# Shifting x in its DMA, loading feed-forward weights during attention, and a layer loop that begins in the feed-forward

## The chip, the cores and the metric

One of the eight cores of a Trainium2 chip runs the kernel. The metric is the device time of one execution in microseconds (us). The kernel before took 2393.64 us (median of three runs, 2389.98 to 2394.75).

## The reference, cut to what matters

x has 16 batches of 128 tokens with 128 features. A cross-attention, a mixture of experts and a second cross-attention come first. The last stage runs six transformer layers; it takes 1840 of the 2383 us, and all that the change touches is there:

```python
def shift_tokens(t):                       # second half of the features comes from the token before
    a, s = jnp.split(t, 2, -1)
    s = jnp.pad(s, ((0, 0), (1, 0), (0, 0)))[:, :-1]
    return jnp.concatenate([a, s], -1)
def attn_layer(x, Wqkv, qs, ksc, Wo):      # 16 heads of 64
    q, k, v = jnp.split(x @ Wqkv, 3, -1)
    q, k = l2norm(q) * qs, l2norm(k) * ksc
    q, k = rotary(q), rotary(k)            # with a scale by position
    return local_attention(q, k, v) @ Wo   # windows of 32, each looks at itself and the window before
def ffn_layer(x, g, bln, W1, b1, W2, b2):
    a, gate = jnp.split((layernorm(x) * g + bln) @ W1 + b1, 2, -1)
    return a * gelu(gate) @ W2 + b2
for i in range(6):
    x = attn_layer(shift_tokens(x), Wqkv[i], q_scale[i], k_scale[i], Wo[i]) + x
    x = ffn_layer(shift_tokens(x), ln_g[i], ln_b[i], W1[i], b1[i], W2[i], b2[i]) + x
```

## The kernel before

The tokens of one batch lie on the 128 partitions; Y holds all 16 batches. The program of each engine is written out by hand, and the engines meet at semaphores only.

**Attention.** A unit is one batch and four heads, 64 units to a layer. A Pipeline (L48) runs the stages of an engine by slots: in slot c, a stage with skew s works on unit c - s, in the order of the list of stages (for TensorE L903: scores, turn_qk, pv, project_qk, project_v, output, turn_o, turn, turn_x). start(...) writes out slots 0 to 7 of a layer, steady() is a hardware loop of seven rounds of eight slots (L73), and finish(...) writes out the last slots. So a layer has 56 slots in the loop and the rest written out.

**x.** For each batch the SyncE queue copies one batch of Y into xin[:, k], k = 0 or 1 (take_x, L363). In slot 4b TensorE turns it (l_turn_x, L796) with two matmuls, each against 64 columns of the array: L802 the first half of the features against the identity, L803 the second half against shift_t, which moves each token one on. It first waits for the copy of v (L1179, ScalarE), which reads the same PSUM bank. ScalarE (L1155) and VectorE (L1571) split the result in two, and the projections (L814, L823) of the next slot read that.

**Values.** ScalarE writes the v of a unit to l_v (L1179). move_values (L349) copies pieces of it to other partitions with four DMAs for two units (L360); pv (L878) of the first of these two units waits for them, some four slots later.

**SyncE's order in a layer** (serve_layer, L372): for each batch move_values for two units, next_x, move_values for the other two. During batches 0 to 2 it loads the six pieces of the next layer's Wqkv. After batch 15 it loads Wo, waits for the first feed-forward group, takes x of batches 0 and 1 for the next layer, waits until the whole feed-forward is done (L400), loads the feed-forward weights of the next layer with twelve DMAs (L335 to L347) and goes back to move_values of batch 0. All of these stand in one queue.

**Feed-forward.** Four groups g of four batches: shift (L919, L920), statistics, normalise (L1653), turn_n (L928), three pairs of hidden matmuls (L944, L945), gelu (L1227), the gated product (L1663), output (L955), residual (L1670). Group 0 begins between the slots of finish(...), and slots 0 to 7 of the next layer's attention (nxt.start) are placed between and after groups 2 and 3. The copy of layer n + 1's first x therefore happens inside the feed-forward of layer n.

**The loop over layers.** On each engine a hardware loop runs layers 0 to 4 (L585 POOL, L1020 TensorE, L1282 ScalarE, L1746 VectorE, L411 SyncE), and its body is rest_of_layer: steady, finish, the feed-forward, nxt.start. It goes back after slot 7 of the next layer, so that the jump lands on that layer's steady(). Layer 5 is written out after the loop: between it and layer 4 no jump is taken. The loop jumps back four times.

Of the kernel before, what the change touches and what calls it, by code (L numbers as in the profile page):

```python
# [90 lines left out]
def build(nc, t, out):  # L91
    with ExitStack() as ctx:
# [193 lines left out]
        def _(sp):  # L286
# [76 lines left out]
            def take_x(ly, b, k):  # L363

                sp.dma_start(xin[:, k], one(Y, b)).then_inc(ld_xin[k], 16)
# [6 lines left out]
            def serve_layer(ly, last):  # L372

                for b in range(4):
                    for q in range(2):
                        move_values(ly, b, b % 2, q)
                        if q == 0:
                            next_x(ly, b, b % 2)
                        if not last and 2 * b + q < W_CHUNKS:
                            if b + q == 0:  # L380
                                sp.wait_ge(l["w_split"], upto(0, (ly + 1) * W_CHUNKS))
                                apart(sp)
                            load_projections(ly + 1, 2 * b + q)
                with sp.Fori(2, B // 2 - 1) as i:
                    for k in range(2):
                        move_values(ly, 2 * i + k, k, 0)
                        next_x(ly, 2 * i + k, k)
                        move_values(ly, 2 * i + k, k, 1)
                for b in range(B - 2, B):
                    for q in range(2):  # L390
                        move_values(ly, b, b % 2, q)
                if not last:
                    sp.wait_ge(l["out_done"], upto(0, (ly + 1) * B))
                    apart(sp)
                    load_output(ly + 1)
                    sp.wait_ge(f["y_done"], upto(0, ly * 4 + 1))
                    apart(sp)
                    for b in range(2):
                        take_x(ly + 1, b, b)
                    sp.wait_ge(f["y_done"], upto(0, (ly + 1) * 4))  # L400
                    apart(sp)
                    load_feed_forward(ly + 1)
# [3 lines left out]
            load_feed_forward(0)  # L406
# [16 lines left out]
        def _(pool):  # L423
# [5 lines left out]
            pool.memset(l_ss[:, :, :, 1:], 1e-24).then_inc(preset, 1)  # L429
# [126 lines left out]
            def feed_forward(ly):  # L556
                fb = ly * 4
                pool.wait_ge(ld_fw, (ly + 1) * (16 * FW_DMAS))
                for g in range(4):
# [11 lines left out]
            def rest_of_layer(ly, att, nxt):  # L571

                att.steady()
                att.finish(0, 1, 2, 3)
                feed_forward(ly)
                if nxt is not None:
                    nxt.start(*range(UNROLL))
# [6 lines left out]
            first.start(*range(2, UNROLL))  # L584
            with pool.Fori(0, LAYERS - 1) as ly:  # L585
                rest_of_layer(ly, attention(ly), attention(ly + 1))
            rest_of_layer(LAYERS - 1, attention(LAYERS - 1), None)


        @block.tensor  # L590
        def _(pe):
# [180 lines left out]
            def attention(ly):  # L772
# [23 lines left out]
                def l_turn_x(u, b, j):  # L796

                    if j % 4 == 0:
                        x = xin[:, j // 4]
                        pe.wait_ge(ld_xin[j // 4], (ly * B + b - j // 4) * 8 + 16)  # L800
                        values_read(l_turn_x, b, 0)
                        pe.matmul(bank[0:HALF, 1, 256:384], x[:, 0:HALF], ident, start=True, stop=True)  # L802
                        pe.matmul(bank[HALF:, 1, 256:384], x[:, HALF:], shift_t, start=True, stop=True)\  # L803
                          .then_inc(l["x_turned"], 1)
# [101 lines left out]
            def feed_forward(ly, last):  # L906
# [54 lines left out]
            def rest_of_layer(ly, att, nxt):  # L961


                shift, turn_n, hidden, output = feed_forward(ly, nxt is None)
# [10 lines left out]
                att.finish(6)  # L975
                for g in range(4):
# [8 lines left out]
                    hidden(g, 1)  # L985
# [33 lines left out]
            first.start(*range(3, UNROLL))  # L1019
            with pe.Fori(0, LAYERS - 1) as ly:  # L1020
                rest_of_layer(ly, attention(ly), attention(ly + 1))
            rest_of_layer(LAYERS - 1, attention(LAYERS - 1), None)


        @block.scalar
        def _(act):
# [205 lines left out]
            def rest_of_layer(ly, att, nxt):  # L1232

# [7 lines left out]
                att.finish(6)  # L1241
                for g in range(4):
# [4 lines left out]
                    gelu(g, 1)  # L1247
# [33 lines left out]
            first.start(*range(3, UNROLL))  # L1281
            with act.Fori(0, LAYERS - 1) as ly:  # L1282
                rest_of_layer(ly, attention(ly), attention(ly + 1))
            rest_of_layer(LAYERS - 1, attention(LAYERS - 1), None)


        @block.vector
        def _(dve):
# [385 lines left out]
            def rest_of_layer(ly, att, nxt):  # L1674

                stats, norm, gated, residual = feed_forward(ly)
# [9 lines left out]
                att.finish(6)  # L1686
                for g in range(4):
# [6 lines left out]
                    if g < 3:  # L1694
# [50 lines left out]
            first.start(*range(3, UNROLL))  # L1745
            with dve.Fori(0, LAYERS - 1) as ly:  # L1746
                rest_of_layer(ly, attention(ly), attention(ly + 1))
            rest_of_layer(LAYERS - 1, attention(LAYERS - 1), None)


# [58 lines left out]
```

## Time and profile before

| | |
|---|---|
| median of three runs | 2393.64 us |
| profiled execution, its own time | 2385.23 us |
| its span, first to last instruction | 2383.4 us |
| mean granted TensorE clock | 0.968 |
| six layers | 545.8 to 2383.4 us |

A layer takes some 307 us from its first projection to the next layer's; 56 slots in the loop take some 211 of them. TensorE is busy for 93% of the span. In the chain of work that ended last, 74% is TensorE's and 4% is time in which an engine waited for nothing that the profile shows ("issue"). In the rows below, "2.44 <-DVE f_n" in brackets is idle time of the engine before the instruction, and what ended it. PE is TensorE's matmul, PEld its weight load, and SPq the queue of SyncE. A matmul in float32 shows as two instructions (x2); a transpose shows as one.

### The profile page before, as it was taken

To read this page: it belongs to the slowest core of one execution; us is meant where nothing else is said; L and a number is where in the kernel's file an instruction comes from. 1 tells how busy PE (TensorE), PEld (TensorE's weight loads), DVE (VectorE), ACT (ScalarE), POOL (GpSimd) and SP (SyncE) were. 2 spreads that over 40 slices of the span, in tenths; PEclk is the share of its full clock that TensorE was granted. 3 is DMA by queue.
4 is the path that set the end of the run, shared out by engine and by line. 5 is a ranking of instruction groups with operands and counts; after the bars stand their busy time and mean duration, and the time that the engine had idled before them with its cause. 6 is when DMAs were issued, how large, how long until landed. Compare 5 with 4: busy or idle time off the path is not lost.

```text
span 2383.4 us, 105405 instructions
## 1 busy us (share of the span) xinstructions
PE 2211.0 (93%) x36645; PEld 1694.9 (71%) x36645; DVE 1725.2 (72%) x4617; ACT 1563.0 (66%) x5192; POOL 1412.3 (59%) x2638
## 2 busy tenths in 40 slices
PE   6998699998999979999799998999988999889998
PEld 4775277776888658886578875788756888578885
DVE  4777788886777657786577865677756788568884
ACT  3554455565888548886478873788746888468883
POOL 3443611115888538885378863688726888278882
PEclk9998899998999989999999999999998999999999
DMA  3000000011111112111111111211102111021110
GB/s 98 0 0 1 0 1 0 0 48 43 49 39 40 31 42 54 40 40 33 43 50 40 40 29 34 63 40 39 34 21 71 40 39 38 14 50 40 40 38 22
DMA packets 107749, 82.51 MB, mean 35 GB/s; under 512 B 26422, under 2 KB 100292, under 8 KB 107588
## 3 DMA queue, kind: packets, MB, share of 16 engines
q1 hardware_dynamic: 107588, 80.46, 12.9%
q8 instruction: 89, 1.46, 0.3%
q14 instruction: 72, 0.59, 0.1%
HBM read 21.94 MB, written 1.05 MB: 10 GB/s over the span
## 4 chain that ended last, share of the span: by engine, by line
PE 74%; DVE 4%; issue 4%; SPq 2%; ACT 1%; POOL 1%; DMA 0%; DVEq 0%; ACTq 0%; POOLq 0%
PE bank L814 14%; PE bank L831 9%; PE bank L898 7%; PE bank L878 6%; PE bank L858 6%; PE bank L823 6%; PE bank L888 4%; PE bank L841 3%; PE bank L850 2%; PE bank L749 2%; PE bank L955 2%; PE bank L944 2%; PE bank L945 2%; PE bank L738 2%; PE bank L597 1%
## 5 line engine op out<-in xcount | busy, mean ns | idle before, releaser
L530 POOL TENSOR_TENSOR l_qk<-l_rot 128x512 f32<-128x512 f32 x384 | 494.4, 1287 | 134.0 <-PE bank L831 60.6
L1202 ACT ACTIVATE l_qkT<-bank 128x512 f32<-128x512 f32 x384 | 229.8, 599 | 278.2 <-PE bank L831 278.2
L1580 DVE TENSOR_TENSOR l_rot<-bank,l_tab 128x512 f32<-128x512 f32 x384 | 265.0, 690 | 197.8 <-ACT l_sq L1186 197.8
L551 POOL TENSOR_TENSOR l_qk<-l_qk,l_rn 128x512 f32<-128x512 f32 x384 | 400.9, 1044 | 0.9
L1166 ACT ACTIVATE prob<-bank,peak 128x64 f32<-128x64 f32 x1536 | 355.0, 322 | 1.3 <-DVE peak L1602 1.3
L814 PE MATMUL bank<-w_high,xs_part 128*128 128x512 f32 x768 | 351.8, 458 | 3.2 <-DVE xs_part L1571 2.8
L1186 ACT ACTIVATE l_sq<-bank 128x512 f32<-128x512 f32 x384 | 237.1, 617 | 55.9 <-PE bank L814 44.8
L1584 DVE TENSOR_TENSOR l_rot<-bank,l_tab 128x512 f32<-128x512 f32 x384 | 261.5, 681 | 0.0
L831 PE MATMUL bank<-const,l_qk 128*128 128x128 f32 x1536 | 255.2, 289 | 5.3 <-POOL l_qk L551 5.2
L1594 DVE TENSOR_REDUCE l_ss<-l_sq 128x8 f32<-128x512 f32 x384 | 259.8, 677 | 0.2
L898 PE MATMUL bank<-l_wo,l_oT 128*128 128x128 f32 x1536 | 239.0, 279 | 0.0
L823 PE MATMUL bank<-w_high,xs_part 128*128 128x256 f32 x768 | 202.9, 286 | 11.6 <-issue 11.6
L878 PE MATMUL bank<-l_v,probT 64*32 64x65 f32 x4608 | 179.5, 225 | 35.2 <-DMA stash<-l_v 22.8
L898 PEld LDWEIGHTS bank<-l_wo,l_oT 128*128 128x128 f32 x1536 | 206.3, 193 | 3.3 <-issue 0.3
L1602 DVE TENSOR_REDUCE peak<-bank 128x4 f32<-128x256 f32 x384 | 160.8, 419 | 50.7 <-PE bank L858 43.4
L831 PEld LDWEIGHTS bank<-const,l_qk 128*128 128x128 f32 x1536 | 163.5, 142 | 41.4 <-POOL l_qk L551 6.8
L878 PEld LDWEIGHTS bank<-l_v,probT 64*32 64x32 f32 x4608 | 117.2, 108 | 105.3 <-issue 105.3
L814 PEld LDWEIGHTS bank<-w_high,xs_part 128*128 128x128 f32 x768 | 146.8, 191 | 62.2 <-issue 5.8
L435 POOL TENSOR_SCALAR ln_rs<-ln_mv 128x1 f32<-128x1 f32 (+1 forms) x64 | 14.5, 227 | 273.5 <-DVE ln_mv L1548 128.3
L858 PE MATMUL bank<-l_qkT 64*32 64x64 f32 x12288 | 175.8, 223 | 0.0
L878 PE MATMUL bank<-stash,probT 64*32 64x65 f32 x7680 | 174.5, 226 | 0.0
L1619 DVE TENSOR_TENSOR o<-bank,rsum 128x256 f32<-128x256 f32 x384 | 163.1, 425 | 13.3
(202 smaller groups left out, 5374.8 us busy)
## 6 DMA issues: line engine op xcount, KB each, us to landing
stash<-l_v SPq DMA_DIRECT2D x768, 65.0 KB, 2.0
early<-in_L_ffn_Wqkv_dram SPq DMA_DIRECT2D x36, 256.0 KB, 3.2
xin<-Y SPq DMA_DIRECT2D x96, 64.0 KB, 1.8
l_wo<-in_L_ffn_Wo_dram SPq DMA_DIRECT2D x6, 512.0 KB, 3.8
f_w<-in_L_ffn_W_dram SPq DMA_DIRECT2D x6, 341.0 KB
out_dram<-X SPq DMA_DIRECT2D x4, 256.0 KB, 2.3
f_w<-in_L_ffn_W_dram SPq DMA_DIRECT2D x6, 128.0 KB
l_oT<-in_L_xattn_Wkv_dram SPq DMA_DIRECT2D x1, 512.0 KB, 6.1
```

The source lines that it names most:

```text
L530: pool.tensor_tensor(l_qk[:, k], l_rot[:, k, 0], l_rot[:, k, 1], ALU.add).then_inc(l["add_done"], 1)
L551: pool.tensor_tensor(v, v, l_rn[:, k, :, None].broadcast_to([128, 8, L_DIM]), ALU.mult).then_inc(l["qk_done"], 1)
L814: ins = pe.matmul(bank[:, 0, :].rearrange("p (q n) -> p q n", q=2), xs_part[:, part, j // 4], w[:, 0:2, 256 * g:256 * g + 256], start=n == ...
L823: ins = pe.matmul(bank[:, 1, 0:256], xs_part[:, part, j // 4], w[:, 2, 256 * g:256 * g + 256], start=n == 0, stop=n == 2)
L831: ins = pe.transpose(bank[:, 2, n * 128:(n + 1) * 128], l_qk[:, j % 2, n * 128:(n + 1) * 128], ident)
L858: ins = pe.matmul(bank[w * WINDOW:(w + 1) * WINDOW, 3 + r, BAND * p:BAND * (p + 1)], l_qkT[rows, j % 2, queries:queries + WINDOW], l_qkT[r ...
L878: ins = pe.matmul(bank[w * WINDOW:(w + 1) * WINDOW, 6 - p, at:at + L_DIM + 1], probT[rows, j % 2, 128 * r + w * WINDOW:128 * r + (w + 1) * ...
L898: ins = pe.matmul(bank[:, 7, 256:384], l_oT[:, j // 4, p], l_wo[:, p], start=p == 0, stop=p == 7, skip_group_check=True)
L1166: ins = act.activation(prob[:, k, n * BAND:(n + 1) * BAND], bank[:, 3 + r, p * BAND:(p + 1) * BAND], ACT.Exp, bias=peak[:, k, n:n + 1])
L1580: dve.tensor_tensor(l_rot[:, k, 0].rearrange("p (q h n) -> p q h n", q=2, h=4), bank[:, 0, :].rearrange("p (q h n) -> p q h n", q=2, h=4), ...
L1584: dve.tensor_tensor(l_rot[:, k, 1].rearrange("p (q h s n) -> p q h s n", q=2, h=4, s=2), bank[:, 0, :].rearrange("p (q h s n) -> p q h s n ...
L1594: dve.tensor_reduce(l_ss[:, k, :, 0], l_sq[:].rearrange("p (h n) -> p h n", n=L_DIM), AX.X, ALU.add)\
```

## The change

It has three parts.

- take_x copies the two halves of the features with a DMA each, and the second half goes to the partition after its own: the shift is done by the DMA. Partition 0 of that half is set to zero once (POOL). l_turn_x becomes one transpose of 128 x 128.
- load_feed_forward(ly) is taken from the end of the layer before (and from the prologue) and stands behind batch 3 of the same layer. The wait for the end of the feed-forward stands before batch 2.
- rest_of_layer is cut in two on TensorE, ScalarE, VectorE and POOL: into_feed_forward (steady, finish and the first part of group 0) and out_of_feed_forward (the rest, and nxt.start). Layer 0's into_feed_forward is written out ahead of the loop; the loop's body is out_of_feed_forward(ly) and into_feed_forward(ly + 1), five rounds; layer 5's out_of_feed_forward follows. The order of the work on each engine stays; the jump back now comes after hidden(0, 1), gelu(0, 1), norm(1) and POOL's part of group 0. SyncE's loop over layers stays where it is.

ScalarE's part of the diff has the same form as TensorE's and is left out.

```diff
@@ -362,7 +362,10 @@
-                sp.dma_start(xin[:, k], one(Y, b)).then_inc(ld_xin[k], 16)
+                x = one(Y, b)
+                sp.dma_start(xin[:, k, 0:HALF], x[:, 0:HALF]).then_inc(ld_xin[k], 16)
+                sp.dma_start(xin[1:, k, HALF:], x[0:S - 1, HALF:]).then_inc(ld_xin[k], 16)
@@ -372,6 +375,9 @@
                 for b in range(4):
+                    if b == 2:
+                        sp.wait_ge(f["y_done"], upto(0, ly * 4))
+                        apart(sp)
                     for q in range(2):
@@ -381,6 +387,7 @@
                             load_projections(ly + 1, 2 * b + q)
+                load_feed_forward(ly)
                 with sp.Fori(2, B // 2 - 1) as i:
@@ -397,13 +404,9 @@
                         take_x(ly + 1, b, b)
-                    sp.wait_ge(f["y_done"], upto(0, (ly + 1) * 4))
-                    apart(sp)
-                    load_feed_forward(ly + 1)
             load_output(0)
-            load_feed_forward(0)
             sp.wait_ge(c["y_done"], upto(0, 2))
@@ -426,7 +429,8 @@
             pool.memset(m_p[:, :, EXPERTS:], -1.0)
-            pool.memset(l_ss[:, :, :, 1:], 1e-24).then_inc(preset, 1)
+            pool.memset(l_ss[:, :, :, 1:], 1e-24)
+            pool.memset(xin[0:1, :, HALF:], 0.0).then_inc(preset, 1)
             pool.wait_ge(preset, 1)
@@ -553,10 +557,9 @@
-            def feed_forward(ly):
+            def feed_forward(ly, *groups):
                 fb = ly * 4
-                pool.wait_ge(ld_fw, (ly + 1) * (16 * FW_DMAS))
-                for g in range(4):
+                for g in groups:
                     yg = Y[:, 4 * g:4 * g + 4, :]
@@ -568,11 +571,14 @@
-            def rest_of_layer(ly, att, nxt):
+            def into_feed_forward(ly, att):
                 att.steady()
                 att.finish(0, 1, 2, 3)
-                feed_forward(ly)
+                pool.wait_ge(ld_fw, (ly + 1) * (16 * FW_DMAS))
+                feed_forward(ly, 0)
+            def out_of_feed_forward(ly, nxt):
+                feed_forward(ly, 1, 2, 3)
                 if nxt is not None:
@@ -582,9 +588,11 @@
             first.start(*range(2, UNROLL))
+            into_feed_forward(0, first)
             with pool.Fori(0, LAYERS - 1) as ly:
-                rest_of_layer(ly, attention(ly), attention(ly + 1))
-            rest_of_layer(LAYERS - 1, attention(LAYERS - 1), None)
+                out_of_feed_forward(ly, attention(ly + 1))
+                into_feed_forward(ly + 1, attention(ly + 1))
+            out_of_feed_forward(LAYERS - 1, None)
@@ -794,14 +802,10 @@
                     if j % 4 == 0:
-                        x = xin[:, j // 4]
-                        pe.wait_ge(ld_xin[j // 4], (ly * B + b - j // 4) * 8 + 16)
+                        pe.wait_ge(ld_xin[j // 4], (ly * B + b - j // 4) * 16 + 32)
                         values_read(l_turn_x, b, 0)
-                        pe.matmul(bank[0:HALF, 1, 256:384], x[:, 0:HALF], ident, start=True, stop=True)
-                        pe.matmul(bank[HALF:, 1, 256:384], x[:, HALF:], shift_t, start=True, stop=True)\
-                          .then_inc(l["x_turned"], 1)
+                        pe.transpose(bank[:, 1, 256:384], xin[:, j // 4], ident).then_inc(l["x_turned"], 1)
@@ -903,7 +907,7 @@
-            def feed_forward(ly, last):
+            def feed_forward(ly):
@@ -958,10 +962,8 @@
-            def rest_of_layer(ly, att, nxt):
-                shift, turn_n, hidden, output = feed_forward(ly, nxt is None)
+            def into_feed_forward(ly, att):
+                shift, turn_n, hidden, _ = feed_forward(ly)
                 att.steady()
@@ -973,6 +975,10 @@
                 att.finish(6)
+                hidden(0, 1)
+            def out_of_feed_forward(ly, nxt):
+                shift, turn_n, hidden, output = feed_forward(ly)
                 for g in range(4):
@@ -982,7 +988,7 @@
                         output(g - 1)
-                    hidden(g, 1)
+                        hidden(g, 1)
                     if g == 3 and nxt is not None:
@@ -1017,9 +1023,11 @@
             first.start(*range(3, UNROLL))
+            into_feed_forward(0, first)
             with pe.Fori(0, LAYERS - 1) as ly:
-                rest_of_layer(ly, attention(ly), attention(ly + 1))
-            rest_of_layer(LAYERS - 1, attention(LAYERS - 1), None)
+                out_of_feed_forward(ly, attention(ly + 1))
+                into_feed_forward(ly + 1, attention(ly + 1))
+            out_of_feed_forward(LAYERS - 1, None)
...
@@ -1671,9 +1684,8 @@
-            def rest_of_layer(ly, att, nxt):
-                stats, norm, gated, residual = feed_forward(ly)
+            def into_feed_forward(ly, att):
+                stats, norm, gated, _ = feed_forward(ly)
                 att.steady()
@@ -1684,6 +1696,10 @@
                 att.finish(6)
+                norm(1)
+            def out_of_feed_forward(ly, nxt):
+                stats, norm, gated, residual = feed_forward(ly)
                 for g in range(4):
@@ -1691,7 +1707,7 @@
                         gated(g, 0)
-                    if g < 3:
+                    if 0 < g < 3:
                         norm(g + 1)
@@ -1743,9 +1759,11 @@
             first.start(*range(3, UNROLL))
+            into_feed_forward(0, first)
             with dve.Fori(0, LAYERS - 1) as ly:
-                rest_of_layer(ly, attention(ly), attention(ly + 1))
-            rest_of_layer(LAYERS - 1, attention(LAYERS - 1), None)
+                out_of_feed_forward(ly, attention(ly + 1))
+                into_feed_forward(ly + 1, attention(ly + 1))
+            out_of_feed_forward(LAYERS - 1, None)

```

## Rows read from the trace of the kernel before

**Rows 1.** The page, part 1: busy time, share, instructions of each engine.

```profile
PE 2211.0 (93%) x36645; PEld 1694.9 (71%) x36645; DVE 1725.2 (72%) x4617; ACT 1563.0 (66%) x5192; POOL 1412.3 (59%) x2638
```

**Rows 2.** Two stretches: engines' busy time, TensorE's clock, DMA share, GB/s.

```profile
930.00:960.00 30.00, 29.83 (x680) 24.11 (x679) 23.96 (x60) 24.37 (x90) 24.51 (x49) 1.00 0.15 40
...
874.00:878.00 4.00, 3.68 (x44) 3.19 (x44) 1.43 (x5) 1.36 (x5) 0.18 (x1) 0.50 0.45 124
```

**Rows 3.** Chain that ended last, in layer 1: start, duration, what.

```profile
904.60 0.39 PE bank L878 x32
...
907.11 0.25 PE bank L802
...
908.67 0.39 PE bank L878 x32
...
912.27 0.39 PE bank L878 x32
```

**Rows 4.** Same stretch in order of time: ScalarE, TensorE's weight loads.

```profile
906.51 0.40 ACT L1179 ACTIVATE l_v<-bank 128x256 f32<-128x256 f32 x1
...
907.04 0.13 PEld L802 LDWEIGHTS bank<-const,xin 128*64 128x64 f32 x1 [0.17 <-ACT l_v L1179]
...
907.41 0.11 PEld L850 LDWEIGHTS bank<-l_mask,cbf 128*128 128x128 bf16 x2 [0.17 <-issue]
...
910.92 0.21 PEld L850 LDWEIGHTS bank<-l_mask,cbf 128*128 128x128 bf16 x2
```

**Rows 5.** The page's groups (busy, mean ns, idle), then the tile xin's landing.

```profile
L831 PE MATMUL bank<-const,l_qk 128*128 128x128 f32 x1536 | 255.2, 289 | 5.3 <-POOL l_qk L551 5.2
...
DMA to landing us min/median/max: 1.8/1.8/4.6
```

**Rows 6.** Waits of TensorE: total us, times, longest.

```profile
PE bank L878 <- DMA stash<-l_v: 22.8, 5, 4.9
...
PE bank L850 <- issue: 15.8, 4, 4.8
```

**Rows 7.** SyncE's queue in order of time, first boundary of layers.

```profile
862.77 0.35 SPq L336 DMA_DIRECT2D f_w<-in_L_ffn_W_dram  x1
...
870.28 1.15 SPq L360 DMA_DIRECT2D stash<-l_v  x2
```

**Rows 8.** TensorE in order of time at layer boundaries, and POOL's L551 there.

```profile
865.85 0.48 PE L814 MATMUL bank<-w_high,xs_part 128*128 128x512 f32 x1
...
874.32 0.28 PE L878 MATMUL bank<-l_v,probT 64*32 64x65 f32 x1 [4.90 <-DMA stash<-l_v]
...
894.10 0.50 PE L814 MATMUL bank<-w_high,xs_part 128*128 128x512 f32 x1
...
1786.99 0.48 PE L814 MATMUL bank<-w_high,xs_part 128*128 128x512 f32 x1
...
1814.61 0.50 PE L814 MATMUL bank<-w_high,xs_part 128*128 128x512 f32 x1
...
2094.27 0.48 PE L814 MATMUL bank<-w_high,xs_part 128*128 128x512 f32 x1
...
2107.45 0.50 PE L814 MATMUL bank<-w_high,xs_part 128*128 128x512 f32 x1
...
2115.16 0.50 PE L814 MATMUL bank<-w_high,xs_part 128*128 128x512 f32 x1
...
L551 POOL TENSOR_TENSOR l_qk<-l_qk,l_rn x4: 1039/1044/1051, 861.0 to 871.0; 128x512 f32<-128x512 f32 x4
```

**Rows 9.** In order of time: layer 0's feed-forward, ScalarE after its jump back.

```profile
821.17 0.66 PE L928 MATMUL bank<-const,f_n 128*128 128x128 f32 x4 [2.44 <-DVE f_n L1653]
...
825.90 1.06 PE L944 MATMUL bank<-f_nT,f_w 128*128 128x512 f32 x2
...
884.97 0.21 ACT L1192 ACTIVATE l_y<-l_s 128x8 f32<-128x8 f32 x1 [2.85 <-issue]
...
887.11 0.39 ACT L1179 ACTIVATE l_v<-bank 128x256 f32<-128x256 f32 x1 [1.94 <-issue]
```

More of the change, by code:

```diff
@@ L1241, in rest_of_layer @@
                 att.finish(6)
+                gelu(0, 1)
+            def out_of_feed_forward(ly, nxt):
+                copy_n, gelu = feed_forward(ly)
                 for g in range(4):
@@ L1246, in rest_of_layer @@
                         gelu(g, 0)
-                    gelu(g, 1)
+                        gelu(g, 1)
                     if g == 3 and nxt is not None:
@@ L1672, in feed_forward, with into_feed_forward @@
                 return f_stats, f_norm, f_gated, f_residual
-            def rest_of_layer(ly, att, nxt):
-                stats, norm, gated, residual = feed_forward(ly)
+            def into_feed_forward(ly, att):
+                stats, norm, gated, _ = feed_forward(ly)
                 att.steady()
@@ L1686, in rest_of_layer, with out_of_feed_forward @@
                 att.finish(6)
+                norm(1)
+            def out_of_feed_forward(ly, nxt):
+                stats, norm, gated, residual = feed_forward(ly)
                 for g in range(4):
@@ L1745, in _ @@
             first.start(*range(3, UNROLL))
+            into_feed_forward(0, first)
             with dve.Fori(0, LAYERS - 1) as ly:
-                rest_of_layer(ly, attention(ly), attention(ly + 1))
-            rest_of_layer(LAYERS - 1, attention(LAYERS - 1), None)
+                out_of_feed_forward(ly, attention(ly + 1))
+                into_feed_forward(ly + 1, attention(ly + 1))
+            out_of_feed_forward(LAYERS - 1, None)
 _INS = ["x", "ctx_1024", "L0_xattn_w_q", "L0_xattn_b_q", "L0_xattn_w_k", "L0_xattn_b_k", "L0_xattn_w_v",
```

## The prediction, made before the changed kernel was run

> **What bounds the kernel now.** I read the page first. TensorE is busy 2211.0 of 2383.4 us [rows 1], and in the middle of a layer it leaves no gap: 29.83 of 30 us, with the other engines at 24 to 24.5 [rows 2]. So there, and only there, each piece of TensorE's time that goes is time of the kernel. The chain that ended last gives the price of a slot. From one start of pv (L878) to the next it is 912.27 - 908.67 = 3.60 us; where the slot turns an x it is 908.67 - 904.60 = 4.07 us [rows 3]. Everything else is found where a layer meets the next. The list of TensorE's waits has two large entries there: L878 waits 22.8 us in 5 places for the DMAs that move v, and L850 waits 15.8 us in 4 places with nothing shown that it waits for [rows 6]. There are five boundaries of layers and four jumps back of the outer loop, and the second wait is the first matmul behind the jump. At the fifth boundary, where no jump is taken, it is absent.
>
> To price a boundary with all its after-effects I take TensorE's order of time from the projection of slot 5 to that of steady slot 1, four slots: 28.25 us at the first boundary (865.85 to 894.10), 27.62 at the fourth (1786.99 to 1814.61), the other two alike (28.29 and 28.14), and 20.89 at the fifth (2094.27 to 2115.16) [rows 8]. The two stalls are less than the excess, since TensorE comes out of them at its lower clock: 0.50 between 874 and 878 us, the 1.2 GHz level, after 4.9 us without a matmul [rows 2, 6].
>
> **Part 1, x is shifted by its DMA: the turn.** The 96 turns (16 batches, six layers) each cost 4.07 - 3.60 = 0.47 us [rows 3]. Where it goes, by the weight loads [rows 4]: an ordinary slot loads L850's weights at 910.92, right behind the last turn of prob. With an x, the load for L802 begins 0.20 us behind that turn's last matmul (906.84, the second of two 0.11 us apart; the same 0.20 in nearly every slot of the loop), the four matmuls take two passes of 0.11 us, as the halves run side by side, and L850's load begins 0.20 us behind the last of them. The view names ScalarE's copy of v as what ended the first gap, but that copy ends at 906.51 + 0.40 = 906.91, and the load comes 0.13 later; so I read both 0.20 as the price of changing from 128 x 128 to 128 x 64 and back. The Trainium skill ("TensorEngine Tiling (Array Packing)", Key Properties) says that a change of tiling mode drains TensorE. The trace agrees, with 0.20 us each way.
>
> A transpose is one instruction and one pass (1536 for 384 units of four [rows 5]) and needs no other shape. Bounds of the saving: 0.11 if both gaps stay and only a pass goes; 0.36 if the new turn costs just its pass. Between them stands the copy of v: it ends at 906.91, and the shortest distance from its end to the load in any turn is 0.05, so the load can begin at 906.96, 0.12 behind an unbroken stream. New price 0.11 + 0.12 = 0.23 us, saving 0.47 - 0.23 = 0.24 us. I take this, since both of its terms are read from the same slot. 96 x 0.24 = **23 us**, bounds 10 and 35.
>
> **Part 1, the DMAs.** Each x now needs two issues on SyncE, one more by about 0.5 us (L360 takes 1.15 for two [rows 7]), with lines of 256 bytes instead of 512. An x is issued some five slots ahead of its turn, 18 us, and lands in 1.8, at worst 4.6 us [rows 5]; even a landing three times as long is covered. The moves of v behind it in the queue are 0.5 us later and needed four slots (14 us) later; in steady slots SyncE has two slots, 7.2 us, for four moves (2.4 us) and two halves of x. Cost 0 for both. POOL's memset is in the prologue, where POOL waits: 0.
>
> **Part 2, feed-forward weights behind batch 3.** At a boundary SyncE waits for the last residual, then issues twelve DMAs from 862.77 on and only at 870.28 the first move of v [rows 7]; TensorE waits 4.90 us, until 874.32 [rows 8]. Afterwards nothing of the kind stands ahead: SyncE goes back as soon as it has issued x of batches 0 and 1, and finds v of units 0 and 1 copied at about 858.5. Four moves to 861 and 2.1 us to land make 863; TensorE wants them at 874.32 - 4.90 = 869.4. The stall goes at five boundaries. What is late next is POOL: it forms L551 for units 0 to 3 every (871.0 - 861.0) / 3 = 3.35 us [rows 8], back to back, and TensorE's slots 5 and 6 can't be shorter. So these two slots take 6.7 (POOL) to 7.2 us (twice 3.60); I take 7.0. The following two take 7.71 at full clock, from 2107.45 to 2115.16 [rows 8]. An undisturbed boundary takes 14.7 us. The fifth boundary has this stall alone: 20.89 - 14.7 = 6.2 us, so the part is worth 5 x 6.2 = **31 us**, bounds 5 x 5.7 and 5 x 6.5.
>
> Moved to behind batch 3, the twelve issues take some 7 us (870.28 - 862.77, less the way round the loop) in a queue which has four to five us to spare in two slots; the moves of batches 4 and 5 come up to 3 us later, against 14 us of cover: 0. The weights are wanted at the end of the layer, over 150 us later. The new wait before batch 2 is for a residual that was done before slot 5: 0. In layer 0 it takes the issues out of the prologue, where SyncE waits anyway: 0.
>
> **Part 3, where the loop begins.** At the four boundaries with a jump, 28.25, 28.29, 28.14 and 27.62 us are left with 20.89 when the jump goes: 7.36 + 7.40 + 7.25 + 6.73 = **28.7 us**. Straight code costs nothing there, by the fifth boundary. But the jump is moved, not removed. The Trainium skill ("Runtime: NRT & Kernel Launch", Instruction fetch mechanics) says that a taken branch whose target isn't held on the chip stops the engine until it is fetched, and that would charge the same in the feed-forward. What would be exposed there: TensorE needs 3.95 us on average, 4.8 at most [rows 6], ScalarE 2.85 and after one instruction another 1.94 [rows 9]; VectorE's fetch is hidden behind TensorE's in the trace, and I put it at ScalarE's two. In the feed-forward TensorE issues hidden(0, 1) and runs out of orders at once: it is done with issuing by 817 us and the next thing, turn_n(1), waits for VectorE's norm until 821.17, with 2.44 us idle [rows 9]. A jump begun at 817 is over by 821 to 822, so it adds 0 to 1 us. ScalarE jumps at about 819 with gelu(0, 1), VectorE at about 820 with norm(1). The first thing that TensorE wants of them is the copy of f_n and gated(0, 1), both for hidden(1, 0) at 825.90 [rows 9]: 6 us against 4.8 for two fetches. POOL has 14 us to spare. I take 0.5 us at each of four jumps, 2 us; bounds 0 and all of it, 28.7 us.
>
> Layers 1 to 5 instead of 0 to 4 now run in the outer loop; five inside and one outside as before: 0.
>
> **Sum.** 23 + 31 + 28.7 - 2 = 80.7 us. The profiled execution took 2385.2 us (span 2383.4), which gives 2304.5. The median of the runs is 8.4 us above it, so 2393.6 - 80.7 = **2313 us**, a ratio of 0.966.
>
> **The rivals.** (a) *The jump is exposed in the feed-forward.* Several engines fetch one after the other, TensorE falls to its lower clock, and all 28.7 us come back instead of 2: 2313 + 26.7 = 2340. For it: ScalarE's double stall [rows 9]. Against it: each engine is idle in that place. 0.13. (b) *The turn saves only a pass*, because the 0.20 us gaps are the wait for the copy of v after all: 10 instead of 23 us, 2326. For it: the releaser named in [rows 4]. Against it: the constant 0.20, and the same gap before L850, which has no such wait. 0.15. (c) *Another wait takes the place of the one for v*, say the Wqkv pieces, which now share the DMA engines with the moves at the same time: 31 us are not gained, 2344. Against it: 6 us of slack. 0.06. (d) *Slower.* The code of the outer loop now lies otherwise; if the eight unrolled slots of TensorE's inner loop no longer stay on the chip together, each of its 42 rounds fetches, at 3.95 us as behind the outer jump (15.8 / 4 [rows 6]): 166 us lost, 2313 + 166 = 2479. It decides from 2 us for each round on (81 / 42), below which the kernel is still faster. Against it: no round does it now (29.83 of 30 us busy [rows 2]), in layers 0 to 4 or in layer 5, whose copies of the loop lie differently, and the loop gets shorter by six instructions for each turn. 0.03. (e) *It doesn't do what it says*: the jump still stalls TensorE at slot 7 or v is still late, for a reason that I don't see; no change, 2393. 0.02. The forecast itself has 0.61.
>
> **How the numbers follow.** The forecast's own bounds are 2313 - 12 - 3 - 2 = 2296 (turn at 35 us, moves at 6.5 us each, no cost of the jumps) and 2330. Up to 2341 the range takes in (a) and (b); it leaves out (c), (d), (e), 11 in 100, and some for what I don't see. Range 2296 to 2341. Within 0.2% is 4.8 us, about what a measurement of this kernel can tell from no change: faster 0.95, same 0.02, slower 0.03.
>
> **What the changed profile would show.** A slot with a turn takes 3.84 us instead of 4.07, 3.96 by (b); the load for the turn begins 0.12 us or less behind the turn of prob, and L850's with no gap. L878's wait for the moves is gone from the list of waits, and so is L850's "issue". The four slots of a boundary take 14.7 us at each of the five. In the feed-forward turn_n(1) is idle for 2.4 to 3.5 us; 6 or more would be (a). TensorE's mean clock rises above 0.968. The prediction is wrong if "issue" waits turn up inside the steady rounds (d), or if slots 5 and 6 take more than 7.2 us each pair (c).

## The result, and the profile after

| | before | after |
|---|---|---|
| median (range) of four runs each | 2391.81 us (2386.86 to 2394.75) | 2299.85 us (2298.88 to 2303.66) |
| profiled execution's span | 2383.4 us | 2297.1 us |
| its own time | 2385.23 us | 2298.88 us |
| mean granted TensorE clock | 0.968 | 0.980 |

The ratio is 0.9621, with a 95% interval of 0.960 to 0.9641. The forecast was 2313 us, with a range of 2296 to 2341.

The page after, part 1 (it answers [rows 1]), then the two groups of part 5 that hold POOL's L551 and TensorE's L831 of before under their new line numbers:

```profile
PE 2163.7 (94%) x36357; PEld 1677.6 (73%) x36357; DVE 1708.3 (74%) x4617; ACT 1555.0 (68%) x5192; POOL 1410.4 (61%) x2639
...
L555 POOL TENSOR_TENSOR l_qk<-l_qk,l_rn 128x512 f32<-128x512 f32 x384 | 400.7, 1044 | 0.9
...
L835 PE MATMUL bank<-const,l_qk 128*128 128x128 f32 x1536 | 252.9, 287 | 6.5 <-POOL l_qk L555 5.8
```

TensorE has 288 instructions fewer (96 turns, three fewer each) and is busy for 47 us less. VectorE and the weight loads are busy for 17 us less each, 1%; ScalarE and POOL are almost the same.

TensorE's waits after (total us, times, longest), against [rows 6]:

```profile
PE bank L932 <- DVE f_n L1666: 22.1, 18, 2.5
...
PE bank L835 <- POOL l_qk L555: 5.8, 7, 4.3
...
PE bank L882 <- issue: 1.9, 5, 0.4
```

Both large entries of before are absent: pv (now L882) waits nowhere for the DMAs of v, and the first matmul of slot 7 (now L854) has no "issue" wait. What leads the list, turn_n waiting for VectorE's norm, was there before as well.

The boundary in layer 1 and the fifth, TensorE in order of time, against [rows 8] (L818 is the projection that was L814):

```profile
859.13 0.48 PE L818 MATMUL bank<-w_high,xs_part 128*128 128x512 f32 x1
...
874.24 0.50 PE L818 MATMUL bank<-w_high,xs_part 128*128 128x512 f32 x1
...
2016.26 0.48 PE L818 MATMUL bank<-w_high,xs_part 128*128 128x512 f32 x1
...
2031.26 0.49 PE L818 MATMUL bank<-w_high,xs_part 128*128 128x512 f32 x1
```

The four slots take 15.11 and 15.00 us, where they took 28.25 and 20.89. The same stretch in a view of stretches (busy time of PE, PEld, DVE, ACT, POOL, granted clock, DMA share, GB/s), first after, then before:

```profile
859.13:874.24 15.11, 13.91 (x331) 11.05 (x329) 11.53 (x29) 12.20 (x45) 12.71 (x27) 1.00 0.29 81
```

```profile
865.85:894.10 28.25, 18.34 (x333) 13.92 (x331) 12.12 (x29) 12.77 (x45) 12.75 (x27) 0.76 0.29 75
```

The work is the same but for the turn, at full clock now (1.00, the 2.4 GHz level) and at 0.76 on average before. TensorE's busy time for it fell by 4.4 us (18.34 to 13.91), on top of the waits that are gone.

Where the 87 us of the six layers went, read from the starts of the first projection matmul of each slot in order of time, in us:

| stretch | before | after | change |
|---|---|---|---|
| 55 slots in the middle of each layer, six layers | 1239.0 | 1212.5 | -26.5 |
| the four boundary slots, five boundaries | 133.2 | 75.3 | -57.9 |
| last projection of a layer to the first of the next, five | 261.2 | 260.4 | -0.9 |
| last feed-forward | 59.3 | 59.5 | +0.2 |
| slots of units 0 to 3 of six layers, and of units 4 to 7 of layer 0 | 140.8 | 138.6 | -2.1 |

A boundary's four slots run from the projection of slot 5 to that of steady slot 1, as in the prediction. They are those of units 4 to 7, since a unit's projection stands one slot behind its number; in the experiments too, "slots 0 to 3" and "slots 4 to 7" count by units. Ahead of the first layer the profiled execution after lost 0.9 us, which leaves 86.3 us between the spans.

The middle of a layer, in the chain that ended last after (start, duration, what), against [rows 3]:

```profile
925.76 0.90 PE bank L818 x3
...
929.66 0.89 PE bank L818 x3
...
931.79 0.15 PE bank L808
...
933.41 0.89 PE bank L818 x3
...
937.00 0.89 PE bank L818 x3
```

From projection to projection there are three sorts of slot. The ordinary one takes 937.00 - 933.41 = 3.59 us, as before. The one with the turn (L808) takes 933.41 - 929.66 = 3.75; the middle value of all of them is 3.77, and was 4.08. The slot behind a round of the inner loop takes 929.66 - 925.76 = 3.90, and was 4.01: this I had not looked at.

ScalarE and TensorE's weight loads in that turn slot, against [rows 4]:

```profile
931.18 0.38 ACT L1187 ACTIVATE l_v<-bank 128x256 f32<-128x256 f32 x1
```

```profile
931.41 0.14 PEld L845 LDWEIGHTS bank<-const,prob 128*128 128x128 f32 x1
931.61 0.14 PEld L808 LDWEIGHTS bank<-const,xin 128*128 128x128 f32 x1
931.68 0.20 PEld L854 LDWEIGHTS bank<-l_mask,cbf 128*128 128x128 bf16 x2
```

The copy of v ends at 931.56. The load for the turn begins 0.05 us later, and the next load 0.07 behind that.

### The profile page after: what moved, and what is told of

The parts are those of the page before. It is cut to its first block, busy times and chain, and to the rows that moved or that the text cites. A ratio compares the mean times of both kernels' runs of the same rounds, so it can differ in the third digit from the quotient of the medians.

```text
span 2297.1 us, 104869 instructions
## 1 busy us (share of the span) xinstructions
PE 2163.7 (94%) x36357; PEld 1677.6 (73%) x36357; DVE 1708.3 (74%) x4617; ACT 1555.0 (68%) x5192; POOL 1410.4 (61%) x2639
## 4 chain that ended last, share of the span: by engine, by line
PE 74%; issue 5%; DVE 4%; POOL 2%; ACT 1%; DVEq 0%; POOLq 0%; ACTq 0%
PE bank L818 14%; PE bank L835 9%; PE bank L902 7%; PE bank L882 6%; PE bank L862 6%; PE bank L827 6%; PE bank L892 4%; PE bank L845 4%; PE bank L757 2%; PE bank L854 2%; PE bank L746 2%; PE bank L949 2%; PE bank L948 2%; PE bank L605 2%; PE bank L959 1%
## 5 line engine op out<-in xcount | busy, mean ns | idle before, releaser
L818 PE MATMUL bank<-w_high,xs_part 128*128 128x512 f32 x768 | 347.4, 452 | 6.0 <-DVE xs_part L1584 5.4
L818 PEld LDWEIGHTS bank<-w_high,xs_part 128*128 128x128 f32 x768 | 144.9, 189 | 63.9 <-DVE xs_part L1584 7.1
L882 PE MATMUL bank<-l_v,probT 64*32 64x65 f32 x4608 | 177.2, 223 | 10.0 <-ACT probT L1182 6.5
L882 PEld LDWEIGHTS bank<-l_v,probT 64*32 64x32 f32 x4608 | 115.4, 106 | 79.1 <-issue 79.1
L882 PE MATMUL bank<-stash,probT 64*32 64x65 f32 x7680 | 172.2, 223 | 0.0
```

The costliest lines, as they stand in the source:

```text
L818: ins = pe.matmul(bank[:, 0, :].rearrange("p (q n) -> p q n", q=2), xs_part[:, part, j // 4], w[:, 0:2, 256 * g:256 * g + 256], start=n == ...
L882: ins = pe.matmul(bank[w * WINDOW:(w + 1) * WINDOW, 6 - p, at:at + L_DIM + 1], probT[rows, j % 2, 128 * r + w * WINDOW:128 * r + (w + 1) * ...
```

## Experiments

In three kernels one part stands alone on the kernel before, in three others one part is taken out of the changed kernel; one kernel changes the turn, and one the place of the work around the jump.

### Part 1 alone

```diff
-                sp.dma_start(xin[:, k], one(Y, b)).then_inc(ld_xin[k], 16)
+                x = one(Y, b)
+                sp.dma_start(xin[:, k, 0:HALF], x[:, 0:HALF]).then_inc(ld_xin[k], 16)
+                sp.dma_start(xin[1:, k, HALF:], x[0:S - 1, HALF:]).then_inc(ld_xin[k], 16)
...
-                        pe.matmul(bank[0:HALF, 1, 256:384], x[:, 0:HALF], ident, start=True, stop=True)
-                        pe.matmul(bank[HALF:, 1, 256:384], x[:, HALF:], shift_t, start=True, stop=True)\
-                          .then_inc(l["x_turned"], 1)
+                        pe.transpose(bank[:, 1, 256:384], xin[:, j // 4], ident).then_inc(l["x_turned"], 1)
```

> The kernel before with part 1 alone (two DMAs for an x, the second shifted; one transpose). Theory: a slot with a turn goes from 4.07 to 3.77 us, as in the changed kernel, all 96 times: 29 us less, about 2363 us, and the stalls at the boundaries stay (22.8 us for the moves of v, 15.8 us of issue). Rival: the turn saves only a pass of 0.11 us, and the rest of the 92 us comes from the boundaries: 10 us less, 2382.

Measured: 2364.04 us (2363.42 to 2368.05) against 2391.11 of before in the same set of runs, ratio 0.9887 (0.9871 to 0.9904), so 27.1 us; the rival's 10 us are ruled out. The turn slot takes 3.77 us, in all layers alike. The 55 middle slots of six layers take 1215.6 instead of 1239.0 us: 23.4 us for 78 turns, 0.30 each. If all turns gain as much, that is 96 × 0.30 = 28.8. TensorE's waits at the boundaries stayed:

```profile
PE bank L878 <- DMA stash<-l_v: 23.7, 5, 6.0
...
PE bank L878 <- ACT probT L1174: 14.8, 10, 2.7
PE bank L850 <- issue: 14.1, 4, 3.7
```

In the profiled execution the five boundaries took 139.0 us, 5.8 more than before, and its span is only 17.2 us shorter. It was the slowest of its four runs, 4.0 us above their median, while the profiled execution of before lay under its own. So what the turn gives can be read from the middle of the layers, where every slot repeats, better than from the span of one execution, in which the boundaries scatter.

### Part 2 alone

```diff
+                    if b == 2:
+                        sp.wait_ge(f["y_done"], upto(0, ly * 4))
+                        apart(sp)
...
+                load_feed_forward(ly)
...
-                    load_feed_forward(ly + 1)
```

> The kernel before with part 2 alone (feed-forward weights behind batch 3). Theory: the wait of L878 for the moves of v goes at all five boundaries, with the slow clock behind it; the issue stall behind the jump stays at four. 31 us less, 2361. Rival: without the other parts the freed time goes into the stall behind the jump or into a slower clock there, and half or less is gained: 2376 or more.

Measured: 2357.60 us (2352.57 to 2358.81), ratio 0.9863 (0.9846 to 0.9879), 33.5 us, 3 more than expected. The wait for the moves of v is gone, and the jump's stall stays:

```profile
PE bank L850 <- issue: 15.4, 4, 4.2
```

The five boundaries take 102.3 instead of 133.2 us: 30.9, of the 31 that the prediction has. The fifth, without a jump, takes 14.87.

### Part 3 alone

```diff
+            into_feed_forward(0, first)
             with pe.Fori(0, LAYERS - 1) as ly:
-                rest_of_layer(ly, attention(ly), attention(ly + 1))
-            rest_of_layer(LAYERS - 1, attention(LAYERS - 1), None)
+                out_of_feed_forward(ly, attention(ly + 1))
+                into_feed_forward(ly + 1, attention(ly + 1))
+            out_of_feed_forward(LAYERS - 1, None)
```

> The kernel before with part 3 alone (the loop over layers begins in the feed-forward). Theory: four boundaries come down from about 28.1 to 20.9 us, as the fifth is, and the jump costs 0 to 1 us each in the feed-forward: 27 to 29 us less, 2364. Rival: the jump is exposed in the feed-forward at 4 us or more with a slow clock behind it, so that the feed-forward (last projection of a layer to the first of the next, 51.6 to 52.4 us) takes 56 us or more and the kernel stays above 2375.

Measured: 2356.68 us (2354.13 to 2361.84), ratio 0.9864 (0.9848 to 0.9881), 34.4 us, where 27 to 29 were expected. Now only the other stall is left:

```profile
PE bank L882 <- DMA stash<-l_v: 19.3, 5, 4.1
```

The four boundaries that had a jump take 21.52, 21.69, 20.77 and 21.41 us, 26.9 less than before. The fifth takes 21.36, 0.5 more than before. The middle of the layers gives 3.3 us as well (1235.7 against 1239.0), although the turn slot is at 4.08.

### Each part taken out of the changed kernel

The diffs are those above, the other way round, against the kernel after.

Without part 1:

```diff
-                        pe.transpose(bank[:, 1, 256:384], xin[:, j // 4], ident).then_inc(l["x_turned"], 1)
+                        pe.matmul(bank[0:HALF, 1, 256:384], x[:, 0:HALF], ident, start=True, stop=True)
+                        pe.matmul(bank[HALF:, 1, 256:384], x[:, HALF:], shift_t, start=True, stop=True)\
+                          .then_inc(l["x_turned"], 1)
```

> The changed kernel without part 1 (x in one DMA, turned by two half-width matmuls, the shift by shift_t). Part 1 alone on the kernel before took 27 us in the runs and only 17 us in the profiled execution, where slots 4 to 7 of the layers 1 to 5 became 6 us longer in all. Theory: that loss belongs to the stall of the moves of v, behind which the second DMA of each x is queued; with parts 2 and 3 in place part 1 is worth its turns alone, 0.30 us x 96 = 29 us, so this kernel takes 2329. Rival: the second DMA costs some us at each boundary in any case; then undoing part 1 costs 20 us or less, 2320.

Without part 2:

```diff
-                load_feed_forward(ly)
...
+                    load_feed_forward(ly + 1)
```

> The changed kernel without part 2 (feed-forward weights ahead of the moves of v again). Theory: the stall of 4 to 5 us comes back at five boundaries with a slow clock behind it, each four slots 21.4 us or more instead of 15.1: 32 to 34 us slower than the changed kernel, 2333. Rival: with the boundary otherwise free, POOL and the moves get ahead and the stall shrinks to 3 us or less without a fall of the clock: 2318.

Without part 3:

```diff
-                into_feed_forward(ly + 1, attention(ly + 1))
...
+                rest_of_layer(ly, attention(ly), attention(ly + 1))
```

> The changed kernel without part 3 (the loop over layers begins at the attention again). Theory: 28 us for the stall behind the jump at four boundaries, as predicted, and 3 us for the slot behind each inner round, which takes 4.01 us again in five layers instead of 3.90: 2331. Rival: the 3.90 belongs to the shorter code of the turn and not to part 3; then rounds stay at 3.90 and the kernel takes 2328; the length of that slot in the trace decides.

| | median (range), us | ratio to before | above the 2299.85 of after |
|---|---|---|---|
| without part 1 | 2328.08 (2327.47 to 2330.52) | 0.9744 (0.9723 to 0.9765) | 28.2 |
| without part 2 | 2328.26 (2323.92 to 2335.16) | 0.9737 (0.9714 to 0.9759) | 28.4 |
| without part 3 | 2334.40 (2333.11 to 2336.24) | 0.9767 (0.9746 to 0.9787) | 34.6 |

The last column compares runs of different sets, so the ratios are the firmer measure: they exceed 0.9621 by 0.0123, 0.0116 and 0.0146, which is 29, 28 and 35 us. Alone the parts gave 27.1 + 33.5 + 34.4 = 95.0, taken out 28.2 + 28.4 + 34.6 = 91.2, and together 92.0. They are additive as far as this can tell: each of these ratios is known to 4 or 5 us either way, so an overlap of a few us would not be seen. Part 1 came out as expected (2329). Taking out part 2 was expected to cost 32 to 34 us and cost 28, in four runs that spread over 11 us, and taking out part 3 cost 3 us more than the 31 expected.

The waits come back as they should. First without part 2, then without part 3:

```profile
PE bank L882 <- DMA stash<-l_v: 21.8, 5, 5.8
```

```profile
PE bank L850 <- issue: 13.9, 4, 3.7
```

Without part 3 the middle of the layers takes 1215.5 us against 1212.5. A slot behind an inner round takes 4.03 us there, and 3.90 after:

```profile
939.19 0.90 PE bank L814 x3
943.22 0.89 PE bank L814 x3
```

So these 3 us belong to part 3. In layer 0, which part 3 writes out ahead of the outer loop, such a slot takes 3.66; in layers 1 to 5 it takes 3.90. In the kernels without part 3 it takes 4.01 in layers 0 to 4 and 3.70 in layer 5. What the kernels differ in there is the form of the layer's number in the waits (a constant, the loop's register, or that plus one). That this is the cause is only argued; no run tries it apart.

### The turn in one step but two passes

The prediction read both gaps of 0.20 us as a change of the array's shape, and set the new turn at one pass of 0.11 and a wait of 0.12. A matmul against the identity turns x just as the transpose does, without a change of shape, in the two passes that a float32 matmul needs.

```diff
-                        pe.transpose(bank[:, 1, 256:384], xin[:, j // 4], ident).then_inc(l["x_turned"], 1)
+                        pe.matmul(bank[:, 1, 256:384], xin[:, j // 4], ident, start=True, stop=True)\
+                          .then_inc(l["x_turned"], 1)
```

> The changed kernel with its transpose replaced by one matmul of 128 x 128 against the identity, which takes two passes as the two half-width matmuls of before did, but needs no other shape of the array. Theory (the change of shape costs 0.20 us each way): a slot with a turn takes 3.77 + 0.11 = 3.88 us, and the kernel is 10 us slower than the changed one, 2310. Rival (the gaps of 0.20 us belong to the passes or to the wait for the copy of v): the slot goes back to 4.07 us and the kernel to 2329.

Measured: 2315.06 us (2311.64 to 2318.46), ratio 0.9687 (0.9669 to 0.9705), 15 us above after. The turn slot takes 3.94 us, between 3.77 and 4.08: neither the 3.88 of the theory nor the 4.07 of the rival. Weight loads in such a slot of this kernel (L808 the turn, L855 the mask):

```profile
935.05 0.30 PEld L808 LDWEIGHTS bank<-const,xin 128*128 128x128 f32 x2
935.27 0.21 PEld L855 LDWEIGHTS bank<-l_mask,cbf 128*128 128x128 bf16 x2
```

The load of L855 now begins 0.22 us behind that of the turn instead of 0.07, so the second pass costs about 0.15 us by the loads and 0.16 by the slot; the other 4.08 - 3.94 = 0.14 us is what the two half-width matmuls with their two changes of shape cost more than one matmul of full width in this place. The 0.30 us of part 1 are thus about 0.16 for a pass and 0.14 for the shape.

Why is that so much less than two gaps of 0.20? TensorE at the mask's matmul, before (its load is in [rows 4]), then in this kernel:

```profile
907.04 0.32 PE L802 MATMUL bank<-const,xin 128*64 128x128 f32 x1
...
907.20 0.27 PE L802 MATMUL bank<-const,xin 128*64 128x128 f32 x1
...
907.41 0.28 PE L850 MATMUL bank<-l_mask,cbf 128*128 128x128 bf16 x2
```

```profile
935.38 0.27 PE L855 MATMUL bank<-l_mask,cbf 128*128 128x128 bf16 x2
```

Of the first gap 0.12 us remains here, as the wait for the copy of v. Of the second, 0.11 us is no loss: in this kernel the mask's load begins 0.11 us ahead of its matmul (935.27 and 935.38), under the matmul before it, while before both begin at 907.41. And the half-width passes begin only 0.16 us apart (907.04 and 907.20), the two passes here 0.21 in the middle of all turns. The middle values give 0.40 - 0.12 - 0.11 - 0.05 = 0.12 us, near the 0.14 of the slots. The Trainium skill ("Perfetto Trace Analysis", Transposes) asks for a transpose instead of an ordinary matmul where one turns data. The runs agree, by 15 us in 96 turns.

### Less cover for the fetch behind the jump

Is the fetch behind the jump gone, or only covered? In the profile after, TensorE in layer 1's feed-forward (L923 and L924 shift, L948 and L949 hidden, L932 turn_n), and the branch of the outer loop (duration min/median/max):

```profile
1098.74 1.02 PE L948 MATMUL bank<-f_nT,f_w 128*128 128x512 f32 x2
1099.60 1.02 PE L949 MATMUL bank<-f_nT,f_w 128*128 128x512 f32 x2
1103.13 0.65 PE L932 MATMUL bank<-const,f_n 128*128 128x128 f32 x4 [2.50 <-DVE f_n L1666]
```

```profile
L1027 PEldq COMPARE_BRANCH  x5: 78/3487/3827, 1098.3 to 2255.1; - x5
```

And the same branch before:

```profile
L1020 PEldq COMPARE_BRANCH  x5: 74/3959/5042, 881.7 to 2108.7; - x5
```

The branch takes almost as long as before, 3.49 us in the middle for 3.96. It begins at 1098.3, while hidden(0, 1) is still in TensorE's queue, and is over at about 1102, before f_n is ready. In the next kernel f_n is ready earlier: the shift of group 1 stands before hidden(0, 0), and VectorE's statistics and norm of group 1 come earlier by as much.

```diff
                 att.finish(4)
+                shift(1)
                 hidden(0, 0)
-                att.finish(5)
-                shift(1)
-                att.finish(6)
+                att.finish(5, 6)
                 hidden(0, 1)
```

> The changed kernel with the feed-forward's shift(1) issued before hidden(0, 0) and its statistics and norm(1) ahead of gated(0, 0) on VectorE, so that turn_n(1) need not wait 2.4 us for norm(1) any more. That wait is also what covers the jump of the outer loop. Theory (the fetch of 4 us stays and was only covered): layers 0 and 5, which take no jump behind it, lose 2 to 2.5 us each in the feed-forward; in layers 1 to 4 TensorE stands as long as before, now with nothing shown that it waits for: 2295. Rival (the jump costs little wherever it stands now): all six layers gain, 6 x 2.4 = 14 us, 2286.

Measured: 2296.44 us (2293.49 to 2299.25), ratio 0.9613 (0.9592 to 0.9635), span 2291.7. TensorE there, its waits for turn_n, and the branch:

```profile
1098.89 1.02 PE L948 MATMUL bank<-f_nT,f_w 128*128 128x512 f32 x2
1099.75 1.02 PE L949 MATMUL bank<-f_nT,f_w 128*128 128x512 f32 x2
1102.49 0.65 PE L932 MATMUL bank<-const,f_n 128*128 128x128 f32 x4 [1.73 <-issue]
```

```profile
PE bank L932 <- issue: 8.2, 5, 2.1
PE bank L932 <- DVE f_n L1665: 8.0, 15, 0.7
```

```profile
L1026 PEldq COMPARE_BRANCH  x5: 67/3507/3949, 1098.8 to 2252.6; - x5
```

VectorE is no longer late by more than 0.7 us, and in the four layers with a jump TensorE now stands there behind its branch, with nothing shown that it waits for: 1.73, 2.12, 1.68 and 2.00 us. In this layer the branch ends at about 1102.3 and turn_n begins at 1102.49. (The fifth of the five "issue" entries, 0.6 us, is in layer 0 ahead of the jumps, and after has it too.) In layers 0 and 5, which take no jump there, the wait of 2.5 us is gone altogether. Layer 0's feed-forward, ahead of any jump, gains 3.1 us (51.88 to 48.75) and the last, behind all jumps, 2.0 (59.47 to 57.50); of the four with a jump three gain 1.3, 0.9 and 1.1 and one loses 0.6, where none was expected to gain. The prediction had weighed the Trainium skill's rule ("Runtime: NRT & Kernel Launch", Instruction fetch mechanics) that a taken branch to code not held on the chip waits for its fetch; the branch's duration agrees, in the old place and in the new. That these 3.5 us are a fetch is the skill's reading; the trace shows their length, and not what is fetched for which engine. They are there at each jump, and the changed kernel hid them in a wait of 2.5 us and the matmuls still queued. This kernel's median is 3.4 us below after's, but the two intervals overlap; that it is faster than after isn't shown.

## Why the prediction was right, and where its sizes were off

The mechanism held in each part. The spans differ by 86.3 us where the sum has 80.7. The medians differ by 92.0, since the profiled execution of before lay 6.6 us under its median and that of after 1.0.

**The turn (23 us predicted; 28.8 by the slots, 27.1 and 28.2 in the runs).** The predicted price of 0.11 + 0.12 = 0.23 us was 0.17 (3.77 - 3.60). The wait was read right: the load begins 0.05 us behind the end of the copy of v, 0.11 behind the turn of prob. The error is in the other term. A pass can't be added in full, since the load of the mask follows 0.07 us behind that of the turn and not 0.11. The reading of before had a flaw of the same kind: two gaps of 0.20 and two passes of 0.11 make 0.62 and not 0.47 us, as the passes begin 0.16 apart and 0.11 of the second gap is no loss. Rival (b), 10 us, is ruled out: the turn slot would have taken 3.96. Its idea was half true, for about 0.12 of the first gap of 0.20 would stay as a wait for v.

**The DMAs of part 1 (0).** After the change the two issues take 0.5 and 0.7 us and no turn waits for xin. The profile shows no landing time for the halves, so how long these DMAs with lines of 256 bytes take isn't shown, only that it is covered.

**Part 2 (31 us; 30.9 in the profile alone, 33.5 in the runs).** The twelve issues stand in SyncE's queue where predicted, in layer 1 from 904.89 on, with the next move of v at 911.40:

```profile
904.89 0.42 SPq L336 DMA_DIRECT2D f_w<-in_L_ffn_W_dram  x1
...
910.49 0.34 SPq L347 DMA_DIRECT2D f_b<-in_L_ffn_b_dram  x1
911.40 2.42 SPq L360 DMA_DIRECT2D stash<-l_v  x4
```

That is 6.5 us for the predicted 7, and pv waits for no move. Rival (c) didn't happen. The lower bound of 5.7 us for a boundary doesn't follow from the rows: 20.89 - 7.2 - 7.71 is 6.0.

**Part 3 (28.7 - 2 = 26.7 us; 34.4 and 34.6 in the runs).** The stall at the four boundaries went, 26.9 us with part 3 alone, and these four are 25.9 us longer when part 3 is taken out. The 2 us for the jump in the feed-forward didn't come: the five feed-forwards between layers take 260.4 us against 261.2. The rival (a), 26.7 us back, is ruled out, and the last experiment shows why it was near: a little less cover, and 1.7 to 2.1 us show at once. About 3 us more came from the slots behind inner rounds, which the prediction hadn't priced at all. It looked at whether the inner loop would refetch (d); it doesn't. Its length for each layer turned out to depend on where the outer loop begins. The rest, up to 34, is not found in single places. With part 3 alone the spans differ by only 31.1 us; the other 3.3 come from how far the two profiled executions lay under their medians (5.9 and 2.6). With part 3 taken out the spans differ by 37.4, of which 3.2 lie ahead of the first layer, where part 3 changes nothing. Slots 0 to 3 of layers 1 to 5 take either 19.0 or 20.3 to 20.6 us in every kernel's profile, in an order that differs from kernel to kernel, and what chooses between the two is open.

**A boundary (14.7 us predicted, 15.0 to 15.1 measured).** The 7.71 us of the second two slots were read at the fifth boundary of before, whose layer stood outside the loop. With a turn 0.30 shorter they should have become 7.4, but took 7.82 (4.06 + 3.76), since the slot at the start of the inner loop takes 4.06 in the loop's form of the code and 3.63 in layer 5 of before. Without part 3, where layer 5 again stands outside, they take 7.38. So "straight code costs nothing there" was wrong: here it is 0.4 us cheaper than the code in the loop. The first two slots took 7.2 to 7.3 and not 7.0, about twice TensorE's 3.60; POOL's 3.35 doesn't show in them. By its own sign, more than 7.2 for these two, the prediction would have called rival (c) in three layers, though no wait for the moves is there; this sign was set too tight.

**The sum.** Turn +5.8, boundaries -3.3 (57.9 measured, of which 1.5 is the turn, for 59.7), jump +2.0, slots behind rounds +3.1, and -2.0 for small things (0.9 ahead of the layers, and turns inside the feed-forward that gained less): 80.7 + 5.6 = 86.3 us. The other 7.4 us between 2313 and 2299.9 come from the base. The prediction carried over the 8.4 us between before's median and its profiled execution; after, this distance is 1.0 us, so this part of the miss is chance: which execution was profiled. I thought that before's scatter (7.9 us from lowest to highest) lay largely in its stalls, which are gone; after has 4.8. That isn't shown: the two-pass kernel, without the stalls too, scatters by 6.8. The range had a slip as well. Its lower bound takes 3 us off for the moves, where 5 × (6.5 - 6.2) is 1.5; the measured median lies above both.

Of the signs named, these came true: no wait of pv for the moves, no "issue" at slot 7, turn_n idle for 2.50 us (2.4 to 3.5 expected), clock 0.980, and the load of the turn 0.11 us behind that of prob. The turn slot at 3.77 undercut the 3.84.

## What to carry to other kernels

Where one engine bounds the kernel, look for the stretches in which its stream is interrupted, and price each by the time between two equal instructions around it: the waits alone (4.9 and some 4 us here) were only two thirds of the 13 us that a boundary lost. A jump back that costs 3.5 us cost nothing here where TensorE had queued work and had to wait for another engine anyway, and whoever shortens that wait uncovers it (1.7 to 2.1 us at a time). And when code moves into or out of a hardware loop, compare slots of the same form of code, since here they differ by 0.1 to 0.4 us (the cause isn't shown).

## What the runs showed of the hardware

- The branch back takes TensorE 3.5 to 4.0 us in the middle at each place tried (3.96 before, 3.49 and 3.51 after it was moved), and the fifth, not taken, under 0.08.
- The slot behind a round of the inner loop costs 0.06 to 0.41 us more than an ordinary one, by the form of code around it: 3.66, 3.70, 3.90, 4.01 against 3.60. Which trait of the form does it isn't shown.
- A change of array shape and back costs about 0.14 us for each turn where part of it lies in a wait, although each gap between loads measures 0.20.
